# Two chosen experts of each token in 15 sorted blocks, and the scan's gelus in pairs

## The reference

```python
logits = xf @ gate_w
top_w, top_idx = jax.lax.top_k(logits, TOP_K)          # 2 of 8
top_w = jax.nn.softmax(top_w)
combine = zeros((t, e)).at[arange(t)[:, None], top_idx].add(top_w)
h = gelu(einsum('td,edf->tef', xf, w1) + b1)           # t tokens, 8 experts, 512 wide
y = einsum('tef,efd->ted', h, w2) + b2
out = einsum('ted,te->td', y, combine)                 # six of eight weights are zero
x = x + gb * out
```

## Time and profile before

| what | us |
|---|---|
| runs, median of 3 (lowest to highest) | 1378.79 (1376.99 to 1382.44) |
| profiled execution, its span | 1379.8 |
| PE busy (matmuls) | 1207.2 (87%) |
| DVE busy | 1037.0 (75%) |
| ACT busy | 852.2 (62%) |
| POOL busy | 489.3 (35%) |
| first row maximum of attention of batch 3 to that of batch 4 | 158.4 |

### The profile page before, as it was taken

One profiled execution on the slowest core, in us unless ns is written; L12 is line 12 of the kernel. 1 busy time (PEld: TensorE's weight loads), 2 busy tenths in 40 slices (PEclk: granted clock), 3 DMA queues, 4 the chain that ended last, 5 costly groups with the idle time before them and its releaser, 6 DMA issues. The chain is left out here.

```text
span 1379.8 us, 19465 instructions
## 1 busy us (share of the span) xinstructions
PE 1207.2 (87%) x6560; PEld 760.5 (55%) x6560; DVE 1037.0 (75%) x2381; ACT 852.2 (62%) x1600; POOL 489.3 (35%) x309
## 2 busy tenths in 40 slices
PE   5974689989998889989999889989899899889698
PEld 3651145655665556555656456655656556555456
DVE  3666977599866997589866997579975998569822
ACT  2634446488646966489565866479664876469332
POOL 0103930078002950069100960049300870029300
PEclk8995579999999999999999999999999999999899
DMA  7101100030001200020001200021000300011000
GB/s 245 70 16 64 60 8 1 16 108 16 16 17 55 69 12 6 16 92 31 17 9 43 88 1 17 16 78 47 16 1 16 109 16 9 1 64 60 8 1 8
DMA packets 18514, 53.22 MB, mean 39 GB/s; under 512 B 4976, under 2 KB 5864, under 8 KB 18032
## 3 DMA queue, kind: packets, MB, share of 16 engines
q1 hardware_dynamic: 16112, 43.40, 9.8%
q0 software_dynamic: 1296, 4.20, 1.0%
q10 hardware_dynamic: 1008, 4.38, 0.8%
HBM read 45.40 MB, written 2.38 MB: 35 GB/s over the span
## 5 line engine op out<-in xcount | busy, mean ns | idle before, releaser
L1482 DVE TENSOR_TENSOR_SCAN probs_T<-bank,probs_T 128x512 f32<-128x512 f32 x256 | 303.9, 1212 | 16.1 <-ACT bank L1078 12.1
L618 PEld LDWEIGHTS bank<-w_w,hidden 128*128 128x128 f32 x2048 | 248.8, 192 | 72.9 <-issue 66.8
L602 PE MATMUL bank<-hT,w_w 128*128 128x512 f32 x512 | 262.9, 629 | 27.1 <-ACT hidden L933 26.2
L447 POOL TENSOR_TENSOR probs_T<-step_space,probs_T 128x1024 f32<-128x1024 f32 x120 | 282.2, 2358 | 5.9 <-DVE probs_T L1482 5.7
L618 PE MATMUL bank<-w_w,hidden 128*128 128x128 f32 x2048 | 251.6, 276 | 2.1 <-DVE expert_sum L1174 1.6
L933 ACT ACTIVATE hidden<-bank,w_b 128x512 f32<-128x512 f32 x256 | 169.6, 686 | 117.5 <-PE bank L602 116.9
L1006 ACT ACTIVATE probs<-bank,row_neg 128x128 f32<-128x128 f32 (+3 forms) x256 | 134.8, 528 | 151.7 <-DVE row_neg L1335 134.8
L1078 ACT ACTIVATE bank<-step_space,a_neg 128x512 f32<-128x512 f32 x256 | 167.8, 683 | 55.0 <-DVE probs_T L1482 36.7
L701 PE MATMUL bank<-k_pad,q_lat 128*128 128x512 f32 (+3 forms) x512 | 185.3, 448 | 5.8 <-DMA k_pad<-xc 5.8
L1335 DVE TENSOR_REDUCE row_neg<-bank 128x1 f32<-128x128 f32 (+3 forms) x256 | 123.5, 487 | 85.1 <-PE bank L703 82.7
L602 PEld LDWEIGHTS bank<-hT,w_w 128*128 128x128 f32 x512 | 89.0, 194 | 153.0 <-ACT hidden L933 97.0
(11 more groups left out here) (183 smaller groups left out, 1577.6 us busy)
## 6 DMA issues: line engine op xcount, KB each, us to landing
probs_T<-b_rows_dram SPq DMA_DIRECT2D x64, 512.0 KB, 3.7
w_w<-in_w_dram ACTq DMA_DIRECT2D x2, 2048.0 KB, 14.0
k_pad<-xc SPq DMA_DIRECT2D x64, 64.0 KB, 2.0
x_in<-in_x_dram POOLq DMA_DIRECT2D x8, 256.0 KB, 3.3
gate<-gate_rows_dram SPq DMA_DIRECT2D x1, 2048.0 KB, 7.0
out_dram<-x_out POOLq DMA_DIRECT2D x7, 256.0 KB, 2.8
step_space<-in_wmod_dram SPq DMA_DIRECT2D x1, 768.0 KB, 5.6
probs_T<-in_wqT_dram SPq DMA_DIRECT2D x1, 512.0 KB, 4.1
```

Source lines behind the costliest of these rows:

```text
L447: ins = nc.gpsimd.tensor_tensor(inject[:, n % 3, :, :], u[:], row.unsqueeze(1).to_broadcast([P, DH, T]), ALU.mult)
L602: mm(hid1_bank(n)[:], w["w1"][:, n // C1, n % C1 * P:(n % C1 + 1) * P], hT[3][:], start=True, stop=True).then_inc(hid1_mm.sem, 1)
L618: ins = mm(to[:, t * P:(t + 1) * P], hidden[:, (e * C1 + c) % (2 * C1), t * P:(t + 1) * P], w["w2"][:, e * C1 + c, :], start=(c == 0), sto ...
L1482: v.tensor_tensor_scan(state[:, n % 2, c, :], decay(DH * n + c)[:], inject[:, n % 3, c, :], 0.0, ALU.mult, ALU.add).then_inc(st_ok.sem, 1)
```

## The change

The second mixture of batches 0 to 6 is computed for the two chosen experts alone; that of batch 7 stays dense. DVE counts how many tokens chose each expert (by small matmuls with triangular matrices, `find_slots` and `place_rows`), gives each expert whole blocks of 128 rows, 15 blocks for any outcome, and gives each (token, choice) a slot. POOL scatters the normalised rows into a DRAM buffer by eight indirect DMAs of 128 rows, SP loads the buffer block by block (`fetch_rows`), PE transposes the blocks, ACT modulates them. For each block SP loads the weights of its expert, 512 KB and 24 KB of bias, into one of four slots of a ring, at an address that it reads from SBUF (`fetch_block`). A block is four 128x128 products into one bank and one bf16 product for the bias (`late_hidden`), one gelu of 512 columns, and four 128x128 products and one bf16 product for the bias (`late_out`). Four blocks are copied out by ACT and saved to DRAM by SP; POOL fetches them back by eight indirect DMAs, weighs, adds and applies the gate (`finish`, formerly on DVE). The expert weights are no longer loaded at the start. The gelus of the scan are two at a time in six detours; ACT's order in the scan gets the copies of outputs.

```diff
+NB = 2 * T // P + E - 1          # 15 blocks
+RING = 4
 sync:
+            def fetch_block(b, j):
+                if j == 0:
+                    sp.wait_ge(blocks_ok.sem, blocks_ok.at(b, 1))
+                e = sp.value_load(block_id[0:1, j:j + 1], min_val=0, max_val=E - 1)
+                n = b * NB + j
+                if n >= RING:
+                    sp.wait_ge(block_mm.sem, n - RING + 1)
+                sp.dma_start(ring[:, ring_slot(n), :], io["experts"][bass.ds(e, 1), :, :]...)
+                sp.dma_start(ring_bias[:, ring_slot(n), :], bias_bf[...][:, bass.ds(e, 1), :]...)
+            def fetch_rows(b):
+                sp.wait_ge(rows_sent.sem, rows_sent.at(b, 16 * 2 * NT))
+                sp.wait_ge(y_mm.sem, y_mm.at(b + 1, 4))
...
+            for b in range(1, B):
+                for j in range(RING):
+                    fetch_block(b - 1, j)
+                fetch_rows(b - 1)
+                if b < B - 1:
+                    place_keys(b + 1)
+                for j in (4, 5):
+                    fetch_block(b - 1, j)
+                save_b(b)
+                spread_rows(b, 0)
+                fetch_block(b - 1, 6)
+                spread_rows(b, 1)
+                spread_rows(b, 2)
+                fetch_block(b - 1, 7)
+                save_outs(b - 1, 0)
+                spread_rows(b, 3)
...
 gpsimd:
+            for b in range(1, B):
+                if b > 1:
+                    get_outs(b - 2)          # 8 indirect DMAs
+                if b < B - 1:
+                    load(b + 1)
+                if b > 1:
+                    finish(b - 2)            # 4 tensor_tensor
+                    store(b - 2)
+                send_rows(b - 1)             # 8 indirect DMAs
                 gate_weights(b)
                 sum_states(b)
-                store(b - 1)
 tensor:
+            def late_hidden(b, j):
+                n = b * NB + j
+                pe.wait_ge(late_act.sem, late_act.at(b, NG + j - 1))
+                pe.wait_ge(*ring_ready(n))
+                for c in range(C1):
+                    mm(to[:, c * P:(c + 1) * P], ring[:, ring_slot(n), c * P:(c + 1) * P],
+                       late_T[:, j * P:(j + 1) * P], start=(c == 0), stop=False, ...)
+                mm(to[:], ring_bias[:, ring_slot(n), :], bias_at_bf[:], start=False, stop=True, ...)
+            def late_out(b, j):
+                pe.wait_ge(late_act.sem, late_act.at(b, NG + j + 1))
+                mm(to, out_bias_bf[0:SPLIT, :], ring_bias[:, ring_slot(n), :], start=True, stop=False)
+                for c in range(C1):
+                    ins = mm(to, hidden[:, LATE_HIDDEN[j % RING], c * P:(c + 1) * P], ring[...], ...)
...
-                early(0, (0, 1))
                 if ahead:
                     project(b + 1, 0)
-                early(0, (2, 3))
-                if ahead:
                     project(b + 1, 1)
...
+                turn(0, 1)                   # 8 transposes, behind the first mixture's hidden products
                 pe.wait_ge(gates_ok.sem, gates_ok.at(b, 1))
...
-                early(1, (0, 1, 2, 3))
-                early(0, out=True)
-                early(2, (0, 1))
+                turn(2, 3)
+                late_h(0)
                 layernorm(b, 2, MISC, (gates_ok.sem, gates_ok.at(b, 1)))
-                early(2, (2,))
+                late_h(1)
                 h_wait(b, 2)
                 for c in range(2 * DH):
                     if c == 2:
-                        early(2, (3,))
+                        late_h(2, 3)
...
-                early(1, out=True, tiles=(0, 1))
+                late_o(0, 1)
...                                      # late_o(2) behind x_proj, late_o(3) behind dt
 vector:
-                early(0) ... early(1) ... early(EARLY_E + SCAN_ADD.index(n))     # all adds, and finish
+            def place_rows(b, mark, link):   # nine small operations at unit 24 of the attention
...
 tables:
-PE_HEAD, ACT_HEAD, DVE_HEAD = (16, 18, 25, 28), (17, 22, 26), (20, 23, 32)
+PE_HEAD, ACT_HEAD, DVE_HEAD = (16, 18, 22), (17, 22), (20, 24, 25)
+SCAN_HIDDEN = {0: (4, 6), 2: (6, 8), 5: (8, 10), 7: (10, 12), 10: (12, 14), 12: (14, 15)}
+SCAN_OUTPUT = {2: (4, 5), 3: (5, 6), 4: (6, 7), 6: (7, 8), 7: (8, 9), 8: (9, 10), 9: (10, 11), 11: (11, 12),
+               12: (12, 13), 13: (13, 14), 14: (14, 15)}
+SCAN_GELU = {3: (4, 6), 8: (6, 8), 13: (8, 10), 18: (10, 12), 23: (12, 14), 27: (14, 15)}
+SCAN_TAKE = {14: 1, 24: 2, 31: 3}
```

More of the change, by code:

```diff
@@ L364, in build @@
         first_a, first_b = FIRST
-        then = [name for name in w if name not in LATE + first_a + first_b]
+        then = [name for name in w if name not in first_a + first_b]
         n_first, n_weights = len(first_a) + len(first_b), len(then)
@@ L399, in spread_rows @@
                 sp.wait_ge(b_saved.sem, b_saved.at(b, 16))
+            def spread_rows(b, p):
                 rows = b_dram[:, :].unsqueeze(0)
[L401 to L413, removed]
+                slot = (p + 2) % 3
+                if p == 1:
+                    sp.wait_ge(dt_l.sem, dt_l.at(b, DH))
+                if p >= 3:
+                    sp.wait_ge(inj_p.sem, inj_p.at(b, 2 * (p - 3) + 3))
+                sp.dma_start(b_wide[:, slot, :, :], rows[:, 2 * p:2 * p + 2, :].to_broadcast([P, 2, T])
+                             ).then_inc(b_rows[p % 3].sem, 16)
@@ L416, in _ @@
+            for e in range(E):
+                fetch(e)
         @block.gpsimd
@@ L607, in out1 @@
+            def out1(n):
                 e, t = divmod(n, NT)
-                to = bank[TAIL_BANK[e][t] if tail else OUT1_BANK[e]]
+                at = ring_slot((B - 1) * NB + e)
+                to = bank[TAIL_BANK[e][t]]
                 if t == 0:
[L610 to L616, removed]
+                    pe.wait_ge(hid1_act, (e + 1) * C1)
+                    if e >= 2:
+                        pe.wait_ge(out1_add, (e - 1) * NT + 1)
@@ L648, in expert_head, with last_gates_T, last_bias @@
                     router(b, 1, w["wg1"])
[L649 to L653, removed]
-                else:
[L655 to L659, removed]
+                else:
+                    find_slots(b)
+            def last_gates_T():
+                pe.wait_ge(last_gates, 1)
+                for t in range(NT):
+                    ins = tr(bank[MISC][0:E, t * P:(t + 1) * P], gates[1][:, t, :], ident[:])
+                ins.then_inc(gt_mm, 1)
+            def last_bias():
+                pe.wait_ge(gt_out, 1)
+                for t in range(NT):
+                    ins = mm(bank[MISC][:, t * P:(t + 1) * P], gates_T[:, t * P:(t + 1) * P], w["b2"][:],
+                             start=True, stop=True)
+                ins.then_inc(b2_mm, 1)
             def sum_first(n):
@@ L680, in main, with turn, late_h, late_o @@
             def main(b, behind, ahead, ending):
-                def early(e, chunks=(), out=False, tiles=range(NT)):
+                def turn(*groups):
                     if behind:
[L685 to L689, removed]
+                        for g in groups:
+                            turn_rows(b - 1, g)
+                def late_h(*blocks):
+                    if behind:
+                        for k in blocks:
+                            late_hidden(b - 1, k)
+                def late_o(*blocks):
+                    if behind:
+                        for k in blocks:
+                            late_out(b - 1, k)
                 def scores(n):
@@ L839, in main @@
                        ).then_inc(in_mm.sem, 1)
-                early(1, out=True, tiles=(0, 1))
+                if behind and ahead:
+                    pe.wait_ge(v_out.sem, v_out.at(b + 1, 1))
+                late_o(0, 1)
                 for c in range(DH):
@@ L961, in expert_head, with take_last_gates, late @@
                     ln_modulate(b, 3, MISC)
[L962 removed]
+                else:
                     route(b, 1)
[L964 to L966 removed]
+            def take_last_gates():
+                act.wait_ge(gt_mm, 1)
+                f(gates_T[:], bank[MISC][0:E, :], ACT.Copy).then_inc(gt_out, 1)
             def iteration(b, behind, ahead):
                 mark, _, check = linker(act, chain_a, b)
[L971 to L974 removed]
+                def late(which, *each):
+                    if behind:
+                        for n in each:
+                            which(b - 1, n)
                 def take_transposed(n):
@@ L1177, in finish @@
[L1177 to L1184 removed]
+                    expert_sum[:, t, :], ALU.mult, ALU.add).then_inc(out1_add, 1)
```

509 lines of the change are left out of this document (362 added, 147 removed).

## The result

The changed kernel takes 1442.70 us (median of 4 runs, 1440.06 to 1446.01) against 1378.92 for the kernel before: 1.0463 times as long, 95% interval 1.0442 to 1.0484. Forecast was 1349. Its profiled execution has a span of 1441.1 us, 61.3 more than the 1379.8 before.

What follows compares the result with a forecast made beforehand. Three limits take turns: PE in attention, PE up to the first convolution, DVE in the scan. Per batch -4.6, seven times -32, +3 setup, -1 tail: -30, giving 1349 us; own range 1325 to 1370, wider range 1300 to 1388.

Steps and rivals of the forecast that it cites:

- The scan's detour: ACT in the scan: two loads and two gelus 3.9 us, 5.3 with decays, against 5.5 covered; 0.4 added.
- The term beside it: Scan start: PE idles some 6 us, state 2's pieces run at half clock, next output row about 1.2 us late.
- the sum's 57.7: Scan length per batch: 55.6 + 0.4 + 1.2 + 0.5 = 57.7 us, against 61.1 before, so -3.4.
- The ring: Expert weights in the scan: block 11's fetch takes 3.7 us to land and comes 0.5 us late.
- The attention: Attention per batch: -0.2 us (-1.3 to +4), with 1.0 charged for POOL's finish beside DVE's layer norm.
- Place of the slot computation: Attention, unit 24: nine DVE operations under 0.3 us each in one block, with 10 us of DVE slack.
- The slower one by the clock: Rival: PE's clock stays low in the scan, +18 us per batch, 1508 us; chance 0.07.
- The one by indirect DMAs: Rival: indirect DMAs hold POOL, rows come late above 2.4 us each, 1490 us at 3.7; chance 0.06.
- the stage to the convolution: Layer norm 2 to first convolution: 8.15 us falls to 5.0, -3.15 per batch (-4.6 to -2.1); 3.5 at full clock.
- the transposes: First mixture, hidden products to gates: eight transposes on PE add 0.6 us per batch (0 to +0.9).
- the conv's late gelus: After the first convolution: gelus of late_h(2, 3) end about 1 us late, +1.0 per batch (0 to +2.6).
- The tail: End of the kernel, once: four adds less before the last mixer, -1 us.

Runs made afterwards that it cites:

- the run with ring and order mended: Changed kernel with ring halves freed and fetched apart, and hidden products of blocks 8, 9, 12, 13 one state earlier: 1372.18 us, ratio 0.9961.
- fetching less: Changed kernel with only an eighth of each block's weights fetched from the second batch on: 1416.19 us, ratio 1.0278.
- fetching sooner: Changed kernel with each ring slot's halves freed and fetched apart, SP's order of issues laid anew, same bytes: 1411.29 us, ratio 1.0236.

## Why the prediction was wrong

- **The scan's detour** is the step that failed first. It took two loads and two gelus as 3.9 us, and with two decays 5.3, inside the 5.5 that the banks cover; in batch 3 it measured 7.17 where 3.9 had been taken. The 3.9 are what the detour takes when its products are ready (3.69 in the run with ring and order mended), and then the scans come to 401 us, 27.5 below before, where I had forecast 24. I priced the instructions of ACT and PE and never laid the two orders side by side: detour 13 opens when scan 10 ends, PE enters state 5 one read product (1.1 us) later and needs 1.08 us for the output row and sum before the first of two hidden products. The term beside it, 1.2 us for the half clock at state 2, was right in kind and not in every batch: DVE waits 1.25 to 1.42 us for the next output row in batches 2, 4 and 5, 0.2 in 1 and 3, and not at all in 6 and 7. The mended scans, 56.5 to 57.8 us, end at the sum's 57.7 or below it.
- **The ring** was in the sum with 0.5 us for block 11, from 3.7 us to land. Blocks 9 and 13 were late, by 1.09 and 2.70: from their last issue to PE's start 639.08 - 633.59 = 5.5 and 663.11 - 656.53 = 6.6 us pass, beside 512 KB of input rows in the same queue:

```profile
633.59 0.55 SPq L484 DMA_DIRECT2D ring_bias<-bias_bf  x1
656.53 0.55 SPq L484 DMA_DIRECT2D ring_bias<-bias_bf  x1
```

  With 3.7 us to land both would have come before PE asked (637.3 against 638.0, 660.2 against 660.4), so the landing is what was mis-sized. Mending the ring alone gave 27 us by fetching less and 31 by fetching sooner. Two of the prediction's own signs, "if PE waits in the scan for a ring DMA by more than 1 us" and "if the attention grows", came true.
- **The attention.** I charged 1.0 us for `finish` beside DVE's layer norm. It costs some 3.3 us of standing and 3.3 of half clock behind it, in five of the six attentions that have it; in batch 4 only the first of the two. The number by the page "SBUF — State Buffer" of the Trainium skill, section "SBUF: two separate sides", all 6.2 us as an exclusive lock, was nearer in size, in part by luck: about half of what it meets is the clock, which that estimate left out. The trace agrees with its rule for two operands in SBUF (0.16 became 1.73 us) and shows the other side of it: row maxima, which read PSUM, keep their 0.69 beside POOL's operation. What I left out was the sequel: DVE's 10 us of slack is a sum, and a stall in front of PE's next transposes is not paid from it. (Of the earlier trace rows the prediction said that DVE's 1.63 us end with POOL's 1.65; they end 0.53 us later, 128.53 against 128.00, so that operation seems to have been held first and to have run then.)
- **Place of the slot computation**: nine operations of 0.15 to 0.36 us where I had under 0.3, but 2.0 us in one piece; batch 1, which has no `finish`, grew by 1.2 us.
- **The rivals.** None had this mechanism. The slower one by the clock had the right sign for a reason that the runs refute: at a mean granted clock of 0.87 to 0.91 the mended scans take 57 to 58 us. The one by indirect DMAs falls: 0.98 to 1.01 us each, as taken, and the last is sent at 565.5, well before the transposes.
- **Right**: the stage to the convolution (3.53 in five batches, the 3.5 that I gave for full clock, and 5.0 and 5.2 at a granted clock of 0.67 in batches 4 and 7, where I had taken 5.0 for all), the transposes (+0.8), the conv's late gelus (smaller than taken), the setup (+2.0 for +3). The tail, forecast at -1, grew by 2.3, and no run says why.

## What to carry to other kernels

Where two engines meet at a point inside a pipeline, price the meeting and not the instructions: write down when the one arrives and when the other is let in, in the order of both queues. A ring buffer's lateness has two parts, when a slot is released and how long the fetch then takes beside other transfers; here the second had grown, and a sooner release covered it. Look for the first reader that could free a part of the slot, and mend that before the order, since a consumer moved earlier onto a late ring can stand in front of its own release. And before moving work to GpSimd, ask which DVE operations with SBUF operands run in those microseconds: a wait that shifts it by some 3 us was worth 30.

## What the runs showed of the hardware

POOL's indirect DMAs take 0.98 us (56 scatters) and 1.01 (56 gathers) of POOL and do not hold DVE: the 128x4 operations beside them stay at 0.15 to 0.17, while beside POOL's arithmetic they wait to its end. DVE's normalising operation, with one tensor operand from SBUF, was held like those with two (four in 3.22 us instead of 1.11).
